# Layers 0, 1 and the first expert sums of a graph network: adjacency stationary, weights applied ahead, node phases inside the next block

## The chip, the cores and the metric

The kernel runs on one core of one Trainium2 chip. The metric is the device time in microseconds of one execution. The kernel before takes 2117.34 us, the median of three runs (2117.11 to 2117.92). Engines are called by the profile's names: PE is TensorE's matmul, PEld its weight load, DVE VectorE, ACT ScalarE, POOL GpSimd, SP SyncE; a name with a q behind it is that engine's sequencer, which issues DMAs and waits for semaphores.

## The reference

3125 nodes with 128 features, 100000 edges from `src` to `dst`. Two graph convolutions come first, then a network of three expert layers.

```python
# reference, shortened
def sage(x, src, dst, W_l, b_l, W_r):
    summed = segment_sum(x[src], dst, 3125)
    cnt = segment_sum(ones, dst, 3125)
    return summed / maximum(cnt, 1.0)[:, None] @ W_l + b_l + x @ W_r
h = relu(sage(x, src, dst, W_l0, b_l0, W_r0))           # layer 0
x = layernorm(x + sage(h, src, dst, W_l1, b_l1, W_r1))  # layer 1

h = x @ W_in + b_in                                     # 128 to 256 features
for l in range(3):                                      # layers 2, 3, 4
    agg = segment_sum(h[src], dst, 3125) / clip(deg, 1.0)
    logits = concat([h, agg]) @ router_W[l] + router_b[l]
    vals, idx = top_k(logits, 2); gates = softmax(vals)  # 2 of 8 experts
    weak = relu(agg @ weak_W[l] + weak_b[l])             # experts 0 to 3
    strong = relu(agg @ strong_W1[l] + strong_b1[l]) @ strong_W2[l] + strong_b2[l]
    moe = sum over the 2 chosen experts of gate * expert(agg)
    h = h + sigmoid(h @ conf_W[l] + conf_b[l]) * moe
return layernorm(x + h @ W_out + b_out)
```

All five layers sum the features of a node's sources over the same edges.

## The kernel before

Nodes are padded to 25 tiles of 128 (S = 25, P = 128). A block is 5 tiles, 640 nodes (TB = 5, BN = 640), and there are 5 blocks (NB = NK = 5).

**Start (to about 389 us).** TensorE multiplies zeros 64 times (L1414). Edges are then ranked by keys (products L1423 to L1427, VectorE L750 to L761), and one-hot products build the adjacency, the count of edges from each source to each target, as bf16 in SBUF (L1450 to L1457, evictions L1264 and L1266).

**Layers 0 and 1.** For each block of 640 target nodes, the adjacency comes in five pieces, each with the sources of five tiles: `ring[:, k, s]` is 128 sources x 640 targets. In layer 0 VectorE and ScalarE lay the pieces out from the adjacency in SBUF (`lay_out`, L407) and SP stores each to the DRAM array `adj_d`; layers 1 and 2 load them from there. The features are fp32, split into three bf16 parts, high, middle and low, which add up to them (`hs`). A part of 128 sources x 128 features is stationary in TensorE, and half of the piece's tile, 320 targets, moves: six sums a source tile, into two PSUM banks (L1480). Layer 0 also needs the number of edges of each target, so a tile of ones is stationary for two more products a source tile (L1485). The aggregate so comes out with the features on the partitions.

After the last sum comes the block's node phase, with TensorE waiting: VectorE forms the reciprocal of the counts over 640 columns (L862 to L864) and scales the sums (L870); TensorE transposes the block's own features (L1523) and multiplies them with W_r and the aggregates with W_l, ten fp32 products (L1531, L1532); VectorE adds the bias, applies the maximum with zero in layer 0, or the residual and layernorm (L920 to L948) in layer 1, and splits the result in three parts. GpSimd stores features and parts to DRAM (`h1_d`, `x1_d`, `split_d`), and the next layer loads the parts from `split_d` before its first sums. The input x is stored to `x_d` and loaded from there a block at a time.

**Layer 2 (first expert sums).** Sums as in layer 1 (L1564), over the 128 features of x. `first_turn` transposes x; `input_block` turns the reciprocals (L1675), forms the router's logits (nine columns, L1678 and L1679) and multiplies with W_in, 256 columns, for the nodes and for the aggregates (L1686). VectorE chooses two experts (L1014 to L1032), the ranks of rows in each expert come from TensorE (L1555), the positions from VectorE (L979 to L993), and GpSimd scatters each node's aggregate twice into rows sorted by expert (L669). VectorE makes the slot tables in the last block (L1076 to L1134).

**Slots and layers 3, 4.** A slot is a group of rows of one expert: SP loads it (L556), TensorE transposes (L1696) and multiplies with the expert's weights (L1707, L1718). The sums of layers 3 and 4 (L1590) have the adjacency as the stationary operand.

Every engine works its own list in the order in which it is written, and waits are semaphores; a waiting instruction holds all behind it on its engine. SP issues loads and stores in the written order.

## Time and profile before

| | us | share of the span |
|---|---|---|
| profiled execution | 2116.81 | |
| its span | 2115.0 | |
| PE busy | 1825.8 | 86% |
| PEld busy | 1473.9 | 70% |
| DVE busy | 904.5 | 43% |
| ACT busy | 775.9 | 37% |
| POOL busy | 627.9 | 30% |

The mean granted TensorE clock is 0.891 of full speed; HBM carries 130 GB/s over the span. Busy shares are means over stages with different limits, so the stages are read apart, by the chain of waits and the timeline. An fp32 matmul shows as two records.

### The profile page before, as it was taken

Reading aid. Unit: us, or ns where it says so; the run is one execution under the profiler, and the core shown is the slowest. Engines: PE = TensorE matmul, PEld = TensorE weight load, DVE = VectorE, ACT = ScalarE, POOL = GpSimd, SP = SyncE. Lnnn points to the kernel's source line nnn. Section 1 sums busy time; section 2 is a strip of 40 time slices with the busy share of each in tenths; the row PEclk is TensorE's granted clock in tenths of the full one; section 3 lists DMA queues with packets and bytes.
Section 4 is the critical chain, followed back from the end, with each engine's and each line's share of the span. In section 5 each row is a group of like instructions: output and inputs, shape, how many; then the busy total and the mean of one; then the engine's idle time right before and its main releaser. Section 6 shows DMA issues by size and latency. Waiting matters only on the chain.

```text
span 2115.0 us, 32510 instructions
## 1 busy us (share of the span) xinstructions
PE 1825.8 (86%) x10660; PEld 1473.9 (70%) x10662; DVE 904.5 (43%) x2470; ACT 775.9 (37%) x1257; POOL 627.9 (30%) x608
## 2 busy tenths in 40 slices
PE   7756666589889799899996999899996998999975
PEld 3545555466667577788885878788885887888864
DVE  6779999553423332543332111443332123433324
ACT  5356666521101010133334565333335554233321
POOL 1234444200000023264442031354440113454430
PEclk7766666799999899899998999899998999899986
DMA  6960000434656786254446753254446742344442
GB/s 151 340 233 0 0 0 0 180 147 162 178 172 239 233 295 206 92 95 73 71 71 193 244 188 101 67 92 73 76 63 222 269 147 97 78 83 73 71 106 63
DMA packets 183593, 277.35 MB, mean 131 GB/s; under 512 B 47551, under 2 KB 152693, under 8 KB 183362
## 3 DMA queue, kind: packets, MB, share of 16 engines
q1 hardware_dynamic: 145186, 217.47, 32.0%
q0 software_dynamic: 38304, 58.53, 15.3%
q8 instruction: 61, 1.00, 0.2%
q14 instruction: 42, 0.34, 0.1%
HBM read 158.82 MB, written 117.13 MB: 130 GB/s over the span
## 4 chain that ended last, share of the span: by engine, by line
PE 76%; DVE 13%; issue 5%; ACT 3%; DMA 2%; DVEq 1%; SPq 0%; POOL 0%; POOLq 0%; ACTq 0%
PE psum L1707 16%; PE psum L1718 16%; PE psum L1590 13%; PE psum L1480 9%; DVE arena L794 7%; PE psum L1564 5%; PE psum L1649 2%; PE psum L1696 2%; PE psum L1457 2%; PE psum L1485 2%; PE psum L1686 1%; PE psum L1425 1%; PE psum L1455 1%; PE psum L1740 1%; DVE arena L863 1%
## 5 line engine op out<-in xcount | busy, mean ns | idle before, releaser
L697 POOL DMA_INDIRECT h_rows<-arena,idx x192 | 310.7, 1618 | 409.6 <-DVE arena L1179 380.4
L1707 PE MATMUL psum<-arena 128*128 128x256 f32 x1536 | 357.4, 386 | 6.0 <-ACT arena L1364 6.0
L1367 ACT ACTIVATE arena<-psum,b1c 128x256 f32<-128x256 f32 x384 | 182.2, 474 | 476.7 <-PE psum L1707 476.5
L1718 PE MATMUL psum<-arena 128*128 x1536 | 347.4, 379 | 0.0
L1707 PEld LDWEIGHTS psum<-arena 128*128 128x128 f32 x1536 | 278.4, 191 | 69.7 <-ACT arena L1367 17.9
L1718 PEld LDWEIGHTS psum<-arena 128*128 128x128 f32 x1536 | 284.6, 190 | 34.8
L794 DVE TENSOR_TENSOR arena<-arena 125x1200 bf16<-125x1200 bf16 (+1 forms) x300 | 282.1, 1007 | 24.9 <-PE psum L1457 24.3
L669 POOL DMA_INDIRECT xs_d<-arena,pos x150 | 145.3, 969 | 407.8 <-DVEq L994 365.7
L1177 DVE TENSOR_TENSOR arena<-psum,arena 128x256 f32<-128x256 f32 x192 | 80.9, 421 | 414.6 <-PE psum L1718 414.6
L1480 PE MATMUL psum<-arena 128*128 128x320 bf16 x1500 | 226.7, 303 | 24.5 <-DVE arena L835 15.8
L623 POOL TENSOR_TENSOR arena<-arena 128x100 bf16 x200 | 134.5, 672 | 245.6 <-ACT arena L1264 241.8
L1480 PEld LDWEIGHTS psum<-arena 128*128 128x128 bf16 x1500 | 148.5, 99 | 84.0 <-issue 24.8
L1590 PE MATMUL psum<-halves,wide_a 128*128 128x512 f32 x625 | 161.3, 402 | 18.4 <-ACT wide_a L1327 17.3
L1590 PE MATMUL psum<-halves,wide_b 128*128 128x512 f32 x625 | 161.5, 403 | 18.1 <-ACT wide_b L1327 17.0
L1266 ACT CAST arena<-psum 128x800 f32 x200 | 165.6, 828 | 0.2 <-issue 0.2
L1590 PEld LDWEIGHTS psum<-halves,wide_a 128*128 128x128 f32 x625 | 114.2, 190 | 41.2 <-issue 19.9
L1590 PEld LDWEIGHTS psum<-halves,wide_b 128*128 128x128 f32 x625 | 114.3, 190 | 40.9 <-issue 19.6
L1457 PEld LDWEIGHTS psum<-arena 125*128 125x128 bf16 x1200 | 122.9, 134 | 24.8
L1457 PE MATMUL psum<-arena 125*128 125x100 bf16 x1200 | 139.7, 270 | 0.0
L1450 PE MATMUL psum<-arena 128*128 128x2 bf16 x200 | 37.4, 187 | 112.9 <-DVE arena L794 92.0
L1450 PEld LDWEIGHTS psum<-arena 128*128 128x128 bf16 x200 | 21.8, 109 | 128.7 <-issue 71.9
L1455 PE MATMUL psum<-arena 125*128 125x200 bf16 (+1 forms) x400 | 108.3, 368 | 0.0
(274 smaller groups left out, 2056.9 us busy)
## 6 DMA issues: line engine op xcount, KB each, us to landing
arena<-adj_d SPq DMA_DIRECT2D x50, 800.0 KB, 6.1
ring<-adj_d SPq DMA_DIRECT2D x50, 800.0 KB, 4.5
xs_d<-zrow SPq DMA_DIRECT2D x8, 3432.0 KB, 26.9
arena<-xs_d SPq DMA_DIRECT2D x96, 264.0 KB, 2.8
adj_d<-arena SPq DMA_DIRECT2D x25, 800.0 KB, 3.3
h_rows<-zrow SPq DMA_DIRECT2D x1, 8192.0 KB, 39.3
h_new<-h_rows SPq DMA_DIRECT2D x12, 640.0 KB, 8.2
arena<-x_d SPq DMA_DIRECT2D x20, 320.0 KB, 3.6
```

Source lines behind the costliest of these rows:

```text
L623: pool.tensor_tensor(a, first_w[:, u % 8], a, ALU.add).then_inc(s_first, 1)
L669: pool.indirect_dma_start(xs_d, bass.IndirectOffsetOnAxis(ap=pos[:, k, t:t + 1], axis=0), pay[:, k, t], None).then_inc(a_scat, 16)
L697: pool.indirect_dma_start(h_rows, bass.IndirectOffsetOnAxis(ap=idx[:, j % 2, h:h + 1], axis=0), ybuf[:, j % 2, h], None, compute_op=ALU.ad ...
L794: v.tensor_tensor(oh, every, keys.rearrange("p (n o z) -> p n o z", z=2, o=1).broadcast_to(shape), ALU.is_equal).then_inc(ready, 1)
L1266: act.copy(adj[:, bass.ds(off[u] + WC, G * WC)].rearrange("p (b n) -> p b n", b=2), banks[:, :, WC:WC + GA]).then_inc(s_wide, 1)
L1367: act.activation(hid[:, j % 2, f], psum[:, 5 + f % 2, 0:M], ACT.Relu, bias=b1c[:, bass.ds(at_b1[j % LOAD] + f, 1)]).then_inc(b_hidf, 1)
L1455: pe.matmul(bank[:, 0:cols], oh1[:, q, n, :, z % 2], ohe[:, q % 2, g, 0:cols, z], start=(z == 0), stop=False, skip_group_check=True)
L1457: mm = pe.matmul(bank[:, bass.ds(rel[(q % 2 * k + g) * (G - NST) + z - NST], WC)], oh1[:, q, n, :, z % 2], oh2[:, q, (g * (G - NST) + z - ...
L1480: mm = pe.matmul(psum[:, h, 0:HN], hs[:, k * SK + s, part, 0:P], half(ring[:, k, s], h), start=(k == 0 and s == 0 and part == 0), stop=(k ...
L1590: return pe.matmul(psum[:, t, :], adj32[piece_no(p, b, k) % 2][:, s, t * P:(t + 1) * P], halves[:, k * SK + s].rearrange("p k f -> p (k f) ...
L1707: mm = pe.matmul(psum[:, 5 + f % 2, 0:M], w1s[:, j % 2, f // 2, kt, f % 2 * P:(f % 2 + 1) * P], xsT[:, j % 2, kt], start=(kt == 0), stop=( ...
L1718: mm = pe.matmul(psum[:, h, 0:H], hid[:, j % 2, f, h * P:(h + 1) * P], w1f[:, bass.ds(at_w2 + f * H, H)], start=(f == 0), stop=(f == FT - 1))
```

## The change

All five parts concern the time before the slots of layer 2.

- **Warm-up:** 110 products of zeros in place of 64.
- **Gather (`gather`, all three layers):** the piece's tile, 128 sources x 128 targets, is stationary, and the three parts of the sources' features move together, 384 columns, into the PSUM bank of the target tile; five banks, one for each tile of the block. In layer 0 a column of ones behind them gives the count (385 columns). ScalarE takes each tile's sums out (`evicted`), in layers 1 and 2 scaled by the reciprocal count; VectorE adds the three parts (`block_of_nodes`).
- **Weights ahead:** for layers 0 and 1 a block's features are transposed (`turn_tiles`) and multiplied with W_l and W_r side by side, 256 columns (`multiply_tile`), before the gather. The left half is split in three parts and gathered; the right half, with the bias, waits in SBUF. In layer 2 the products have W_in and the router's ten columns, 266.
- **Node phases inside the next block:** the transposes and products are cut in three stages, which `beside` puts behind the source tiles named in PLACES (piece, tile), for the layer of which the block's nodes are made. The first two blocks of nodes of layer 0 go ahead of its first sums, the other three between the pieces of its first block.
- **No DRAM between:** parts stay in SBUF (`parts0`, `parts1`, used in turn); `split_d`, `h1_d` and `x_d` go. x comes in five chunks, VectorE lays out four of the first five pieces (FIRST_DVE), and rows to be scattered have two buffers in layer 2 (`pay_of`). The early part of the slot tables comes one block sooner.

```diff
+FIRST_DVE = (0, 2, 3, 4)
...
+        parts0 = carve([S, FW], BF16)
+        sums = carve([TB, FW], F32)
+        turned4 = carve([4, P], F32)
+        rest = carve([TB, D], F32)
         assert used[0] <= BN * SK * NK
+        used[0] = BN * SK * NK
+        parts1 = carve([S, 3 * D], BF16)
+        z1 = carve([S, D], F32)
+        assert used[0] <= 2 * BN * SK * NK
+        features = (parts0, parts1, parts0)
...
+            for k in range(NK):
+                for o, i in x_rows(chunk(x_all, k), k):
+                    sp.dma_start(o, i).then_inc(s_x[k], 16)
+                if k == 0:
+                    for o, i in ((wlr[0][:, 0:D], Wl0), (wlr[0][:, D:2 * D], Wr0)):
+                        sp.dma_start(o, i).then_inc(s_w0, 16)
...
-            def split_in(p):
...
-                pool.dma_start(split_d[:, bass.ds(b * TB, TB), :, 0:D].rearrange("p t k d -> p (t k) d"),
...
+            def products_split(n, t):
+                u = unit(n, t)
+                z = chunk(z0 if n < NB else z1, n % NB)
+                bank = psum[:, 6 + u % 2]
+                v.wait_ge(n_high, u + 1)
+                if n and t == 0:
+                    v.wait_ge(n_feat, n)
+                v.tensor_tensor(z[:, t], bank[:, D:2 * D], bl_b, ALU.add)
+                v.tensor_tensor(rest[:, t], bank[:, 0:D], parts_of(n)[:, t, 0], ALU.subtract).then_inc(n_taken, 1)
+            def low_part(n):
+                v.wait_ge(n_mid, n + 1)
+                v.tensor_tensor(parts_of(n)[:, :, 2], rest, parts_of(n)[:, :, 1], ALU.subtract).then_inc(n_feat, 1)
+            def block_of_nodes(p, b):
+                here, r = chunk(z0 if p == 0 else z1, b), rcol[:, b * TB:(b + 1) * TB]
+                a = sums[:, :, 0:D]
+                v.wait_ge(n_out, TB * (NB * p + b + 1))
+                if p == 0:
+                    d = sums[:, :, 3 * D]
+                    link(v.tensor_scalar(deg[:, 0], d, 1.0, None, ALU.max))
+                    link(v.reciprocal(deg[:, 1], deg[:, 0]))
+                    link(v.scalar_tensor_tensor(r, d, 1.0, deg[:, 1], ALU.min, ALU.mult))
+                link(v.tensor_tensor(sums[:, :, D:2 * D], sums[:, :, D:2 * D], sums[:, :, 2 * D:3 * D], ALU.add))
+                link(v.tensor_tensor(a, a, sums[:, :, D:2 * D], ALU.add))
+                if p == 0:
+                    for t in range(TB):
+                        ins = v.scalar_tensor_tensor(a[:, t], a[:, t], r[:, t:t + 1], here[:, t], ALU.mult, ALU.add)
+                    link(ins)
+                    link(v.tensor_scalar(a, a, 0.0, None, ALU.max))
+                elif p == 1:
+                    link(v.tensor_tensor(a, a, here, ALU.add))
+                    v.wait_ge(s_ldr, 16 * (b + 1 + (b == NB - 1)))
+                    link(v.tensor_tensor(rblk, rblk, a, ALU.add))
+                    layernorm(b)
+                v.nop().then_inc(n_node, 1)
...
+                    if b == (NB - 2 if p == 2 else NB - 1):
...
+            def evicted(i, t):
+                act.wait_ge(s_agg, TB * i + t + 1)
+                if i < NB:
+                    act.copy(sums[:, t, 0:3 * D + 1], psum[:, t, 0:3 * D + 1]).then_inc(n_out, 1)
+                else:
+                    c = i % NB * TB + t
+                    act.activation(sums[:, t, 0:3 * D], psum[:, t, 0:3 * D], ACT.Copy, scale=rcol[:, c:c + 1]).then_inc(n_out, 1)
...
-            for _ in range(64):
+            for _ in range(110):
...
-                    def summed(k, h, s):
-                        for part in range(3):
-                            mm = pe.matmul(psum[:, h, 0:HN], hs[:, k * SK + s, part, 0:P], half(ring[:, k, s], h),
-                                           start=(k == 0 and s == 0 and part == 0), stop=(k == NK - 1 and s == SK - 1 and part == 2))
...
+            def turn_tiles(n, g):
+                source = chunk(x_all, n) if n < NB else sums[:, :, 0:D] if n < 2 * NB or n >= 3 * NB else rblk
+                if 2 * n + g:
+                    pe.wait_ge(n_turned, 2 * n + g)
+                if n < NB:
+                    pe.wait_ge(s_x[n], 32 if n == NB - 1 else 16)
+                else:
+                    pe.wait_ge(n_node, n - NB + 1)
+                for t in ((4,) if g else range(4)):
+                    mm = pe.transpose(psum[:, 5, t % 4 * P:(t % 4 + 1) * P], source[:, t], ident[:, :])
+                mm.then_inc(n_turn, 1)
+            def multiply_tile(n, t):
+                u = unit(n, t)
+                weights = wlr[n // NB] if n < 2 * NB else w_ins[:, n // NB - 2, 0:H + 10]
+                pe.wait_ge(n_turned, 2 * n + 1 + t // 4)
+                if u >= 2:
+                    pe.wait_ge(n_taken, u - 1)
+                pe.matmul(psum[:, 6 + u % 2, 0:weights.shape[1]], turned4[:, t % 4], weights, start=True, stop=True).then_inc(n_mult, 1)
+            def turned_and_multiplied(n, stage):
+                if stage == 0:
+                    turn_tiles(n, 0)
+                elif stage == 1:
+                    multiply_tile(n, 0)
+                    turn_tiles(n, 1)
+                    multiply_tile(n, 1)
+                else:
+                    for t in range(2, TB):
+                        multiply_tile(n, t)
+            PLACES = (((1, 1), (1, 4), (2, 4)), ((2, 4), (3, 2), (3, 4)), ((0, 4), (1, 1), (1, 4)))
+            def gather(p, b):
+                i = NB * p + b
+                width = 3 * D + (1 if p == 0 else 0)
+                def summed(k, s, t):
+                    return pe.matmul(psum[:, t, 0:width], ring[:, k, s, t * P:(t + 1) * P], features[p][:, k * SK + s, 0:width],
+                                     start=(k == 0 and s == 0), stop=(k == NK - 1 and s == SK - 1))
...
+                for k in range(NK):
+                    if p == 0:
+                        pe.wait_ge(s_rel[k], b + 1)
+                        if b == 0 and k < NK - 1:
+                            if k:
+                                for stage in range(3):
+                                    turned_and_multiplied(k + 1, stage)
+                    else:
+                        pe.wait_ge(s_ring[k], (NB * (p - 1) + b + 1) * 16)
+                    pe.wait_ge(n_feat, NB * p + k + 1)
+                    if k < NK - 1:
+                        for s in range(SK):
+                            for t in range(TB):
+                                if i and k == 0 and s == 0:
+                                    pe.wait_ge(n_out, TB * (i - 1) + t + 1)
+                                mm = summed(k, s, t)
+                            if s == SK - 1:
+                                mm.then_inc(s_piece, 1)
+                            beside(k, s)
+                    else:
+                        for t in range(TB):
                             for s in range(SK):
...
+                                mm = summed(k, s, t)
+                            mm.then_inc(s_agg, 1)
...
+            pe.wait_ge(s_ones, 1)
+            for n in range(2):
+                for stage in range(3):
+                    turned_and_multiplied(n, stage)
+            for b in range(NB):
+                gather(0, b)
...
-                        first_aggregate(b)
-                        first_turn(b)
-                        input_block(b)
+                        gather(2, b)
...
+                    for stage in range(3):
+                        turned_and_multiplied(4 * NB - 1, stage)
```

Named in the rows below are the lines of the changed kernel: L1455 is `turn_tiles`, L1464 `multiply_tile`, L1484 `gather`. TensorE's order at the start of layer 0, before:

```order
L1495 REGISTER_ALU [waits aggregates_taken]
L1480 MATMUL psum<-arena 128x320 [waits x_split,piece_laid_out_0]
L1480 MATMUL psum<-arena 128x320 x5
L1485 MATMUL psum<-arena,ones_s 128x320 x2
L1480 MATMUL psum<-arena 128x320 x6
```

and after the change:

```order
L1455 MATMUL psum<-ident,arena 128x128 [waits count_columns_set,new_windows_copied,x_in_0,first_weights_in,tables_ready]
L1455 MATMUL psum<-ident,arena 128x128 x3
L1464 MATMUL psum<-arena 128x256 [waits turned_tiles_taken]
L1455 MATMUL psum<-ident,arena 128x128 [waits x_in_0,turned_tiles_taken]
L1464 MATMUL psum<-arena 128x256 [waits turned_tiles_taken]
L1464 MATMUL psum<-arena 128x256 [waits products_taken,turned_tiles_taken] x3
L1455 MATMUL psum<-ident,arena 128x128 [waits x_in_1,turned_tiles_taken]
...
L1464 MATMUL psum<-arena 128x256 [waits products_taken,turned_tiles_taken] x4
L1484 MATMUL psum<-arena 128x385 [waits features_ready,piece_laid_out_0]
L1484 MATMUL psum<-arena 128x385 x24
L1455 MATMUL psum<-ident,arena 128x128 [waits x_in_2,turned_tiles_taken,piece_laid_out_1]
```

The sums stood first; now ten transposes and ten products stand before them, and five more of each behind the first piece of 25 sums. TensorE's order in a block of layer 2, before (L1635 transposes of x, L1675 turned reciprocals, L1678 and L1679 logits, L1686 products with W_in), from the last piece on:

```order
L1564 MATMUL psum<-arena 128x320 [waits splits_in_4,piece_in_4]
L1564 MATMUL psum<-arena 128x320 x29
L1635 MATMUL psum<-ident,arena 128x128 [waits expert_residual_in]
L1635 MATMUL psum<-ident,arena 128x128 x4
L1675 MATMUL psum<-ident,arena 128x1 [waits router_products_taken,expert_aggregates_taken,turned_taken]
L1675 MATMUL psum<-ident,arena 128x1 x4
L1678 MATMUL psum<-arena 128x9
L1679 MATMUL psum<-arena 128x9
...
L1686 MATMUL psum<-arena 128x256 x5
L1686 MATMUL psum<-arena 128x256 [waits node_major_groups_taken]
```

and after, from the first piece of the second block of layer 1 on, in which the first block's nodes are made:

```order
L1484 MATMUL psum<-arena 128x384 [waits sums_evicted,features_ready,piece_in_0]
L1484 MATMUL psum<-arena 128x384 [waits sums_evicted] x4
L1484 MATMUL psum<-arena 128x384 x20
L1484 MATMUL psum<-arena 128x384 [waits features_ready,piece_in_1]
L1484 MATMUL psum<-arena 128x384 x24
...
L1455 MATMUL psum<-ident,arena 128x128 [waits nodes_ready,turned_tiles_taken,router_products_taken]
L1455 MATMUL psum<-ident,arena 128x128 x3
L1484 MATMUL psum<-arena 128x384 [waits features_ready,piece_in_3]
L1484 MATMUL psum<-arena 128x384 x14
L1464 MATMUL psum<-arena 128x266 [waits products_taken,turned_tiles_taken]
L1455 MATMUL psum<-ident,arena 128x128 [waits nodes_ready,turned_tiles_taken]
L1464 MATMUL psum<-arena 128x266 [waits products_taken,turned_tiles_taken]
L1484 MATMUL psum<-arena 128x384 x10
L1464 MATMUL psum<-arena 128x266 [waits products_taken,turned_tiles_taken] x3
L1484 MATMUL psum<-arena 128x384 [waits features_ready,piece_in_4]
```

The node phase stood behind all sums; now the transposes stand behind 15 source tiles of the next block and the products behind 18 and 20. On VectorE, the end of a layer-0 block before (L862 to L864 reciprocals of the counts, L870 scaling, L875 bias, L878 maximum):

```order
L862 TENSOR_SCALAR arena<-psum 128x320 [waits banks_aggregated]
L863 RECIPROCAL arena<-arena 128x320 [waits vector_steps]
L864 SCALAR_TENSOR_TENSOR arena<-psum,arena 128x320 [waits vector_steps]
L862 TENSOR_SCALAR arena<-psum 128x320
L863 RECIPROCAL arena<-arena 128x320 [waits vector_steps]
L864 SCALAR_TENSOR_TENSOR arena<-psum,arena 128x320 [waits vector_steps]
L870 TENSOR_TENSOR arena<-psum,arena 128x320 [waits aggregates_taken,banks_aggregated] x2
L407 COPY arena<-arena 128x640 [waits banks_aggregated,piece_stored_4]
L407 COPY arena<-arena 128x640 x4
L875 TENSOR_TENSOR arena<-psum,arena 128x384 [waits items_for_vector]
L875 TENSOR_TENSOR arena<-psum,arena 128x256 [waits items_for_vector]
L878 TENSOR_SCALAR arena<-arena 128x640 [waits items_taken_by_vector]
```

and after (L810 to L812 reciprocals, L813 and L814 the three parts added, L817 scaling, L819 maximum):

```order
L810 TENSOR_SCALAR deg<-arena 128x5 [waits piece_laid_out_3,piece_laid_out_4,piece_laid_out_2,sums_evicted,piece_laid_out_1,piece_laid_out_0]
L811 RECIPROCAL deg<-deg 128x5 [waits vector_steps]
L812 SCALAR_TENSOR_TENSOR rcol<-arena,deg 128x5 [waits vector_steps]
L813 TENSOR_TENSOR arena<-arena 128x5x128 [waits vector_steps]
L814 TENSOR_TENSOR arena<-arena 128x5x128 [waits vector_steps]
L817 SCALAR_TENSOR_TENSOR arena<-arena,rcol 128x128 [waits vector_steps]
L817 SCALAR_TENSOR_TENSOR arena<-arena,rcol 128x128 x4
L819 TENSOR_SCALAR arena<-arena 128x5x128 [waits vector_steps]
L408 COPY arena<-arena 128x640 [waits vector_steps,tiles_aggregated,piece_stored_4]
```

The reciprocals shrink from 320 columns twice to 5, and the additions of the three parts are new.

## Rows read from the trace of the kernel before

**Rows 1.** The page, chain that ended last: its shares by engine.

```profile
PE 76%; DVE 13%; issue 5%; ACT 3%; DMA 2%; DVEq 1%; SPq 0%; POOL 0%; POOLq 0%; ACTq 0%
```

**Rows 2.** Chain of waits, pieces in order of time: start us, us, what.

```profile
586.94 22.75 PE psum L1480 x150
...
686.10 20.38 PE psum L1480 x150
...
721.13 3.58 PE psum L1547 x16
...
893.60 3.80 PE psum L1707 x16
901.48 3.52 PE psum L1707 x16
...
1148.14 30.10 PE psum L1590 x125
```

**Rows 3.** Timeline, start of layer 0: start, busy us, instructions, [idle before, releaser].

```profile
389.03 4.14 DVE L407 COPY arena<-arena 128x640 bf16<-128x640 bf16 x15 [5.29 <-ACT arena L1266]
...
403.41 1.76 PE L1480 MATMUL psum<-arena 128*128 128x320 bf16 x6 [15.75 <-DVE arena L835]
```

**Rows 4.** Timeline, warm-up and the first two rounds of keys.

```profile
2.27 16.70 PE L1414 MATMUL psum<-arena 128*128 128x512 bf16 x63 [2.27 <-POOL arena L606]
...
30.44 0.59 PE L1423 MATMUL psum<-arena 1*125 1x400 bf16 x1 [11.47 <-DVE arena L750]
...
46.12 0.57 DVE L761 TENSOR_TENSOR arena<-psum,arena 125x400 f32<-125x400 f32 x1 [13.03 <-PE psum L1427]
...
54.70 0.57 DVE L761 TENSOR_TENSOR arena<-psum,arena 125x400 f32<-125x400 f32 x1 [0.91 <-PE psum L1427]
```

**Rows 5.** Windows: length, busy (x) of the five engines, PEclk, DMA share, GB/s.

```profile
18.00:20.00 2.00, 0.97 (x5) 0.24 (x3) 2.00 (x1) 2.00 (x1) 0.00 (x0) 1.00 0.13 6
20.00:22.00 2.00, 0.00 (x0) 0.00 (x0) 1.90 (x4) 2.00 (x1) 0.00 (x0) 0.86 0.11 3
...
470.00:472.00 2.00, 2.00 (x11) 2.00 (x11) 0.16 (x2) 0.00 (x0) 0.00 (x0) 0.50 0.60 253
...
752.00:778.00 26.00, 26.00 (x175) 19.27 (x174) 9.01 (x46) 2.75 (x3) 4.75 (x6) 0.94 1.06 368
```

**Rows 6.** Instruction groups by line: | busy us, mean ns | idle before, releaser.

```profile
L1480 PEld LDWEIGHTS psum<-arena 128*128 128x128 bf16 x1500 | 148.5, 99 | 84.0 <-issue 24.8
...
L1264 ACT CAST arena<-psum 128x100 bf16<-128x100 f32 x200 | 48.8, 244 | 119.5 <-PE psum L1457 117.7 <-POOL arena L623 0.2
...
L1177 DVE TENSOR_TENSOR arena<-psum,arena 128x256 f32<-128x256 f32 x192 | 80.9, 421 | 414.6 <-PE psum L1718 414.6
```

**Rows 7.** Timeline, products at the end of layer 0's first block.

```profile
435.88 0.49 PE L1531 MATMUL psum<-arena 128*128 128x128 f32 x2 [2.78 <-DVE arena L870]
```

**Rows 8.** Timeline, VectorE at the end of a layer-1 block.

```profile
638.31 0.82 DVE L920 TENSOR_TENSOR arena<-arena 128x640 f32<-128x640 f32 x1
...
641.47 1.37 DVE L948 TENSOR_SCALAR arena<-arena 128x128 f32<-128x128 f32 x5
```

**Rows 9.** The page, DMA issues: xcount, KB each, us to landing.

```profile
arena<-x_d SPq DMA_DIRECT2D x20, 320.0 KB, 3.6
```

**Rows 10.** Timeline, end of layer 2 and start of the slots.

```profile
867.66 0.17 DVE L1076 TENSOR_TENSOR arena<-nxt,cap 128x8 f32<-128x8 f32 x1
...
868.35 0.98 POOL L669 DMA_INDIRECT xs_d<-arena,pos  x1 [15.56 <-DVEq L994]
...
875.85 0.16 DVE L1134 TENSOR_SCALAR arena<-arena 1x12 int32<-1x12 f32 x1
...
883.01 20.26 SPq L556 DMA_DIRECT2D arena<-xs_d  x4
...
891.01 0.66 PE L1696 MATMUL psum<-ident,arena 128*128 128x128 f32 x4 [0.93 <-DVE arena L1061]
```

**Rows 11.** Timeline, one of the last products of the kernel.

```profile
2088.84 4.63 PE L1740 MATMUL psum<-arena 128*128 128x128 f32 x20 [0.46 <-ACT arena L1406]
```

816 lines of the change are left out of this document (328 added, 488 removed).

## The prediction

> **What bounds the kernel now.** I read the chain of waits by engine first, then its pieces in order of time, then the stages between them in the timeline. The chain is 76% TensorE [rows 1], so a microsecond is won where TensorE stands idle, streams columns that need not exist, or runs at its lower clock. The pieces give the stages [rows 2]: layer 0 runs until layer 1 starts at 586.94, layer 1 until about 710, layer 2 (the first expert sums) from 721.13, and the slots of the first expert layer start at 893.60. Layer 0 starts at 403.41, when the first MATMUL follows 15.75 us of idle [rows 3]. So the three gathering layers take 893.60 - 403.41 = 490.2 us. Behind 893.60 the change alters nothing that costs time (semaphores and places of buffers only), so that part is to move as a block.
>
> **The key stage (64 to 110 warm-up matmuls).** TensorE warms up from 2.27 to 18.97, then idles 11.47 us and starts the keys at 30.44; the first of four rounds ends at 46.12, the second 8.58 us later, at 54.70 [rows 4]. The first lasts 15.7 us, since the granted clock is at its lower level when it starts: it was 1.00 in 18 to 20, and fell within 20 to 22 (mean 0.86, so some 2.4 us after the last matmul) [rows 5]. 46 matmuls more of 512 columns, at 2.4 GHz 213 ns each, end at about 28.8; the gap shrinks to 1.6 us, less than the 2.4 us that the clock lasted. The first round then takes 8.6 instead of 15.7: 7.1 us are won, since VectorE and ScalarE wait for TensorE in it. If the clock falls anyway, 0. I take 7.1.
>
> **The gather.** Before, a piece of five source tiles takes per tile six sums and, in layer 0, two counts of 320 columns. In layer 1, 150 sums take 20.38 us: 135.9 ns for one [rows 2], which is 320 columns at 2.4 GHz (133.3) and 2.6 ns. After, a block is 125 matmuls of 384 columns (385 in layer 0, the last is the count): 162.6 to 163 ns, 20.4 us. Layers 1 and 2 gain nothing from it (750 x 320 = 625 x 384 columns); layer 0 loses its 250 counts. The weight load has a mean of 99 ns [rows 6], under 163, and stays hidden.
>
> The Trainium skill, page "TensorE: Matmul & The Clock Gate", section "Back-to-back issue gap", has a rule that would give more: in a stream of load and matmul pairs, 81 ns at 128 columns and 131 ns at 512. Interpolated, 384 columns would take about 114 ns, and 1875 of them 92 us less than below. By the same rule 320 columns would take 106 ns; the trace has 135.9, so the trace disagrees and the sum goes by it.
>
> **The node phase.** In layer 1 a block lasts 24.2 us: the chain's pieces end at 586.94 + 22.75 and 686.10 + 20.38, four blocks apart [rows 2]. So its node part costs TensorE 3.8 us: five transposes, ten fp32 products of 128 columns, and short waits. The new node part has the same columns (five transposes, five products of 256 or 266), placed in three stages inside the next block. It costs 3.8 again if nobody is late. In layer 0 the old node part costs more: VectorE's reciprocals over 640 columns hold TensorE 2.78 us [rows 7], and these go (the new one has 5 columns). In layer 2 five blocks and the end took 893.60 - 721.13 = 172.5, or 34.5 each: nine-column products, twenty products of 256 columns, and waits.
>
> Who might be late: layer 0, TensorE wants the tiles after seven source tiles, 7 x 0.82 = 5.7 us. Last eviction 0.6, three small steps 0.6, two adds over 640 columns 2 x 0.86, five tiles 1.4, the maximum 0.5: ready at about 4.9, slack 0.8. Layer 1, wanted after 15 tiles, 12.2: eviction 0.7, three adds 2.6, then the residual add and layernorm, which take 638.31 to 642.84 = 4.5 before [rows 8]: 7.8, slack 4. Layer 2, wanted at 4.1: 0.7 and 2 x 0.86, slack 1.6. The third product stage waits about 0.5 us for banks 6 and 7 in every block; that is inside the 3.8, as the old waits were. What is queued behind a late stage is the whole next piece of sums, and behind a late ScalarE the next evictions.
>
> So a block is 20.4 + 3.8 = 24.2; without any wait 23.3, and with 2 to 3 us of late chains 27.
>
> **Layer 0, start.** VectorE now lays out four of five pieces: 20 copies at 4.14/15 = 0.276 [rows 3], ready at 394.5. The first chunk of x, 320 KB, issued at 391.4, takes 3.6 us as such a block does now [rows 9], the weights are queued behind: about 396. Then two blocks of nodes go through turn, copy, product, high part, two VectorE steps, all exposed and at the lower clock. Transposes and their copy 2.0; then per tile a product (a warm record of 256 columns is 3.52/16 = 0.22, two records a tile, cold 0.9 [rows 2]), a cast (0.24) and two VectorE steps (0.55, from 0.42 for 256 columns) [rows 6]; two banks, so two tiles per round trip: 5.4 from the first product. Block 0 of nodes: 396 to 403.4; the second 8.0: TensorE gathers from 411.4, against 403.4: 8 us lost (bounds 5 and 14).
>
> Block 0 then has three more such stages in it, which TensorE walks through in order. Each is 5.6 us at the upper clock: transposes and copy 1.5, and 4.1 for the five products with their round trips. Sums: 4.1 a piece, 6.1 for the first, half of it cold as now. 6.1 + 3 x (5.6 + 4.1) + 4.1 = 39.3, and 1.5 for short falls of the clock: 40.8, until 452.2. Bounds 34 and 60.
>
> **Layer ends.** No store, load or split lies between layers any more: features are made block by block, four pieces ahead. Layer 0: 4 x 24.2 = 96.8, until 549.0. Layer 1: 5 x 24.2 and the 16 nine-column records, now 3.58 us cold [rows 2], warm half, with a switch 2.3: 123.3, until 672.3. Layer 2: 5 x 24.2 and 2.0 for ranks and the ten columns more: 123.0, until 795.3. The expert weights go out behind the pieces of block 1, and the pieces for block 2 queue behind them. Both together, 9.6 MB, took 26 us at 368 GB/s from 752 to 778 [rows 5]; they are wanted in pieces over 24 to 40 us: hidden.
>
> **The end of layer 2.** The last ranks stand 4.1 us before the gather ends. VectorE then takes 1.8 for the positions and 8.4 for the slot tables (867.66 to 876.0) [rows 10], so it is free 6.1 us behind the end, and two adds make the nodes ready at 7.9. Turn, copy, five cold products: 14.5. The other limit is the scatter: now from 868.35 to the load of sorted rows at 883.01, 14.7 [rows 10]; the new one starts 2.3 before the end, so the load goes at 12.4 and rows are in at about 15.5. The slot's first transposes follow, and the first product 2.6 later (891.01 to 893.60): 18 us, until 813.3. Bounds 15 and 22.
>
> **The sum.** 813.3 - 893.6 = -80.3, and -7.1 at the keys: -87.4. The profiled execution took 2116.81 with a span of 2115.0; 2116.8 - 87.4 = 2029.4. The median of the runs is 0.5 above it, so 2030.
>
> **Rivals.**
> 1. Block 0 runs cold. The stages with gaps between them keep TensorE half busy. For: the final projections, with gaps between them, run 20 records of 128 columns in 4.63 us, the lower clock [rows 11], and behind the same gap of the next block the clock stood at 0.50 (470 to 472) [rows 5]. Against: pieces of 4.1 us full work lie between, and the clock rose within 4 us of them at 403. Price: 125 sums at twice 163 are 20 us more, 15 products 6 more, less 3.5 already counted, and some of it warm: +18, 2048. Chance 0.17.
> 2. The node chains are late. The slack in layer 0 is 0.8 us by a sum of ten steps, each with a semaphore, and ScalarE lays out a piece between two turned copies. At 2 us in each of 14 blocks: +28, 2058. Chance 0.13.
> 3. The clock falls before the keys: +7, 2037. For: the gap is not zero. Chance 0.08.
> 4. Matmuls of 384 columns go as fast as their weight loads: 99 ns [rows 6] instead of 163, 1875 x 64 = 120 us less, 1910. Against: loads of 99 ns stand beside 135.9 ns for 320 columns [rows 2, 6]. The rule of the Trainium skill quoted above lies on this side, with its 114 ns. Chance 0.01.
> 5. Slower than before: with the adjacency stationary, each of 1875 matmuls pays its own weight load. If none is hidden, 99 ns x 1875 = 186 us, 2216; it decides from 47 ns a matmul. For: layers 3 and 4, in this orientation, take 30.10/125 = 241 ns for 512 columns [rows 2], 27 above 213. Against: that load is fp32, and the bf16 loads of 99 ns vanish under 136 now. Chance 0.03.
> A plan that does less than it says (a feature or piece late by a cycle of waits) has 0.02 more, somewhere up to 2110.
>
> **How the numbers follow.** The sum has 0.56: 2030, its own range 2014 to 2046, from the bounds above (start -3 to +6, block 0 -7 to +10, blocks -10 to +12, end -3 to +4, not all at once). The range of 8 in 10 takes in rivals 1 and 3 and most of 2: 2012 to 2060. A measurement tells 0.2% (4 us) from no change. Faster holds in all cases but rival 5 and a part of the last: 0.96; within 0.2%: 0.01; slower 0.03.
>
> **What would show it.** In the new profile: the first key round 8.6 us instead of 15.7; the first 385-column matmul about 1 us after 404 (411 less 7); block 0 of 41 us with three gaps; then 14 blocks of 24 us, each 125 matmuls at 163 ns, TensorE busy 95% or more and at clock 1.00; no gap between layers; 18 us from the last sum to the first slot's product; slots at 7.41 us apart as before. Wrong would be: matmuls at over 170 ns; TensorE waits for nodes_ready or features_ready of a microsecond or more in every block; a clock of 0.5 in block 0; a slower slot stage.

## The result, and the profile after

The changed kernel takes 2049.68 us, the median of four runs (2040.57 to 2053.5), against 2117.63 before: ratio 0.9656, 95% interval 0.9624 to 0.9687. Forecast were 2030, with a range of 2012 to 2060. So 68 us are won where 87 were forecast: inside the range of the forecast, above the 2014 to 2046 that its sum gave itself. The profiled execution took 2050.06 with a span of 2048.1 and a granted clock of 0.898 (before 0.891).

The page of the changed kernel, the chain's shares by engine [rows 1] and the gather's groups:

```profile
PE 76%; DVE 12%; issue 5%; ACT 3%; DMA 2%; DVEq 1%; SPq 1%; POOL 0%; ACTq 0%; POOLq 0%
...
L1484 PE MATMUL psum<-arena 128*128 128x384 bf16 (+1 forms) x1875 | 318.2, 327 | 0.5 <-ACT arena L1233 0.2
...
L1484 PEld LDWEIGHTS psum<-arena 128*128 128x128 bf16 x1875 | 181.9, 98 | 126.6 <-ACT arena L1236 3.3
```

TensorE is idle before its sums for 0.5 us in all, so the 1875 loads of 98 ns stand beside its matmuls. The pieces of the chain (start, us, what) that answer to [rows 2]:

```profile
416.22 4.09 PE psum L1484 x25
...
474.09 14.03 PE psum L1484 x85
...
498.14 14.03 PE psum L1484 x85
...
599.77 4.71 PE psum L1484 x29
...
623.54 4.71 PE psum L1484 x29
...
814.99 6.57 PE psum L1657 x16
825.65 3.52 PE psum L1657 x16
```

A piece of 25 sums takes 4.09, 163.6 ns each. Blocks are 24.05 us apart in layer 0 and 23.77 in layer 1. The stages, by where they end (before, forecast from the prediction's sum, after):

| end of | before | forecast | after | stage, forecast | stage, measured |
|---|---|---|---|---|---|
| adjacency (first layout copy starts) | 389.03 | 381.9 | 393.25 | -7.1 | +4.2 |
| node blocks ahead (first sum) | 403.41 | 404.3 | 416.06 | 22.4 | 22.8 |
| block 0 of layer 0 | | 445.1 | 452.8 | 40.8 | 36.7 |
| layer 0 | 586.94 | 541.9 | 554.5 | 96.8 | 101.7 |
| layer 1 | | 665.2 | 675.2 | 123.3 | 120.7 |
| layer 2's sums | | 788.2 | 795.1 | 123.0 | 119.9 |
| first slot product starts | 893.60 | 806.2 | 814.99 | 18.0 | 19.9 |
| span | 2115.0 | 2027.6 | 2048.1 | 1221.4 | 1233.1 |

Three rows carry the miss: the adjacency stage (11.3 us), layer 0 (4.9), and all that stands behind the first slot product (11.7), which was to move as a block. The other five together are 7.5 us shorter than forecast. The end of a layer is read from the eviction of its last sums (ScalarE, start us, busy us); in the timeline of the changed kernel these are the last ones of layers 0, 1 and 2:

```profile
554.48 0.48 ACT L1233 COPY arena<-psum 128x385 f32<-128x385 f32 x1 [0.34 <-PE psum L1484]
...
675.19 0.58 ACT L1236 ACTIVATE arena<-psum,rcol 128x384 f32<-128x384 f32 x1 [0.23 <-PE psum L1484]
...
795.12 0.58 ACT L1236 ACTIVATE arena<-psum,rcol 128x384 f32<-128x384 f32 x1 [0.24 <-PE psum L1484]
```

For block 0 of layer 0 it is the end of TensorE's last sum, 444.43 + 8.37 = 452.8, since ScalarE evicts late there: it lays out pieces of block 1 first.

```profile
444.43 8.37 PE L1484 MATMUL psum<-arena 128*128 128x385 bf16 x50
...
446.08 6.36 ACT L408 COPY arena<-arena 128x640 bf16<-128x640 bf16 x10
...
452.35 1.99 ACT L1233 COPY arena<-psum 128x385 f32<-128x385 f32 x5
```

The gain lies in two stretches of the table. Layer 0, from its first sum to its end, took 183.5 us before and takes 138.4; from there to the first slot product were 306.7 and are 260.5. Against these 91.3 us stand 4.2 more for the adjacency, 8.4 more ahead of the first sum and 11.7 more behind the first slot product. No run tests the turned gather or the missing trips to DRAM alone, so how the 91.3 divide between the parts of the change is read from the stages and not shown by experiment, but for the placing of the node phases.

**The keys.** Windows of the changed kernel (columns as in [rows 5]):

```profile
30.00:32.00 2.00, 1.69 (x9) 1.14 (x9) 2.00 (x7) 1.71 (x1) 0.00 (x0) 1.00 0.40 3
32.00:34.00 2.00, 2.00 (x8) 1.25 (x7) 0.95 (x3) 2.00 (x1) 0.00 (x0) 0.58 0.42 3
...
58.00:60.00 2.00, 2.00 (x8) 1.41 (x7) 0.00 (x0) 0.00 (x0) 0.00 (x0) 0.59 1.09 341
```

Its timeline, the first key product and VectorE's steps behind the first and the second round [rows 4]:

```profile
30.31 0.38 PE L1397 MATMUL psum<-arena 1*125 1x400 bf16 x1 [2.84 <-DVE arena L710]
...
44.85 0.57 DVE L721 TENSOR_TENSOR arena<-psum,arena 125x400 f32<-125x400 f32 x1 [11.89 <-PE psum L1401]
...
60.41 0.57 DVE L721 TENSOR_TENSOR arena<-psum,arena 125x400 f32<-125x400 f32 x1 [7.90 <-PE psum L1401]
```

The warm-up ended at 27.47, 1.3 sooner than forecast, the gap was 2.84 us and the keys started at the upper clock. But the clock fell at about 32.3, when TensorE was busy again, and came back at about 59.6 although TensorE was busy throughout: two rounds at the lower clock instead of one.

**Block 1 of layer 0.** The first product of layer 1's features, in the timeline of the changed kernel:

```profile
459.91 2.62 PE L1484 MATMUL psum<-arena 128*128 128x385 bf16 x15
...
465.00 0.70 PE L1464 MATMUL psum<-arena 128*128 128x256 f32 x2 [2.48 <-DMA arena<-in_L_gnn_b_l]
...
466.33 5.68 PE L1484 MATMUL psum<-arena 128*128 128x385 bf16 x25
```

It waits 2.48 us for layer 1's bias, which SP issues at 460.69, behind the wait for the layouts of this block. The clock falls behind the wait (0.95 in 464 to 466, 0.50 in 466 to 468), and 25 sums take 5.68 instead of 4.25.

**The end of layer 2**, timeline of the changed kernel [rows 10]:

```profile
803.29 1.09 PE L1455 MATMUL psum<-ident,arena 128*128 128x128 f32 x4 [8.21 <-DVEq L825]
...
809.35 1.58 SPq L530 DMA_DIRECT2D arena<-xs_d  x3
...
812.23 0.66 PE L1646 MATMUL psum<-ident,arena 128*128 128x128 f32 x4 [1.56 <-DMA arena<-xs_d]
...
814.99 6.57 PE L1657 MATMUL psum<-arena 128*128 128x256 f32 x16 [2.11 <-ACT arena L1338]
```

TensorE waits 8.21 us for the last block's nodes (forecast 7.9), and the slots start 19.9 us behind the last sum. Its first slot runs at the lower clock: 10.66 us to the next instead of 7.88 before.

**The slots.** Weight loads in the timeline of the changed kernel, around one slot's transposes (L1646):

```profile
877.69 1.70 PEld L1657 LDWEIGHTS psum<-arena 128*128 128x128 f32 x8
879.58 1.59 PEld L1657 LDWEIGHTS psum<-arena 128*128 128x128 f32 x8 [0.20 <-ACT arena L1341]
881.60 0.42 PEld L1646 LDWEIGHTS psum<-ident,arena 128*128 128x128 f32 x4 [0.42 <-issue]
```

Before, nearly every slot's first product came 7.41 us behind the last slot's; now every fourth comes 7.65 behind. That slot is the one before which TensorE loads four addresses from the slot tables into registers. In the order of instructions nothing had changed there.

### The profile page after: what moved, and what is told of

It reads as the page before. It is cut to its first block, busy times and chain, and to the rows that moved or that the text cites. A ratio compares the mean times of both kernels' runs of the same rounds, so it can differ in the third digit from the quotient of the medians.

```text
span 2048.1 us, 30902 instructions
## 1 busy us (share of the span) xinstructions
PE 1787.7 (87%) x9855; PEld 1380.5 (67%) x9858; DVE 892.3 (44%) x2593; ACT 829.3 (40%) x1388; POOL 618.4 (30%) x593
## 4 chain that ended last, share of the span: by engine, by line
PE 76%; DVE 12%; issue 5%; ACT 3%; DMA 2%; DVEq 1%; SPq 1%; POOL 0%; ACTq 0%; POOLq 0%
PE psum L1657 17%; PE psum L1668 16%; PE psum L1484 14%; PE psum L1571 13%; DVE arena L754 7%; PE psum L1623 2%; PE psum L1464 2%; PE psum L1646 2%; PE psum L1431 2%; PE psum L1399 2%; PE psum L1429 1%; PE psum L1690 1%; PE psum L1617 1%; ACT wide_b L1317 1%; ACT wide_a L1317 1%
## 5 line engine op out<-in xcount | busy, mean ns | idle before, releaser
L1484 PE MATMUL psum<-arena 128*128 128x384 bf16 (+1 forms) x1875 | 318.2, 327 | 0.5 <-ACT arena L1233 0.2
L754 DVE TENSOR_TENSOR arena<-arena 125x1200 bf16<-125x1200 bf16 (+1 forms) x300 | 282.0, 1006 | 23.6 <-PE psum L1431 23.0
L1484 PEld LDWEIGHTS psum<-arena 128*128 128x128 bf16 x1875 | 181.9, 98 | 126.6 <-ACT arena L1236 3.3
L1103 DVE TENSOR_TENSOR arena<-psum,arena 128x256 f32<-128x256 f32 x192 | 80.9, 421 | 381.9 <-PE psum L1668 380.8
L1424 PEld LDWEIGHTS psum<-arena 128*128 128x128 bf16 x200 | 21.6, 108 | 126.7 <-issue 81.2
## 6 DMA issues: line engine op xcount, KB each, us to landing
xs_d<-zrow SPq DMA_DIRECT2D x8, 3432.0 KB, 27.3
```

Source lines behind the costliest of these rows:

```text
L754: v.tensor_tensor(oh, every, keys.rearrange("p (n o z) -> p n o z", z=2, o=1).broadcast_to(shape), ALU.is_equal).then_inc(ready, 1)
L1484: return pe.matmul(psum[:, t, 0:width], ring[:, k, s, t * P:(t + 1) * P], features[p][:, k * SK + s, 0:width], start=(k == 0 and s == 0), ...
```

## The experiments

**130 warm-up matmuls.**

```diff
-            for _ in range(110):
+            for _ in range(130):
```

> The changed kernel with 130 warm-up matmuls in place of 110. In the changed kernel the warm-up ends at 27.46 us, TensorE idles 2.84 us, the keys start at 30.31 at the full clock, the clock falls at about 32.3 and is back only at about 59, so the first key round takes 14.5 us and the second 15.6 instead of 8.6 each. Theory: the idle gap makes the clock fall, although it falls after the gap. With 20 more matmuls (20 x 0.213 = 4.3 us) there is no gap, the first round ends at about 39 and all rounds take 8.6: 5.9 + 7.0 = 12.9 us less, 2037. Rival: the clock falls because of what the keys do (their products use 100 of 128 rows, and few rows in the first), gap or not: then it falls again at about 32 and the time stays at 2050.

Measured: 2044.42 (2041.47 to 2046.59), ratio to before 0.9634 (0.9605 to 0.9664), so some 5 us less and not 13. Windows of its trace:

```profile
32.00:34.00 2.00, 2.00 (x11) 1.31 (x11) 1.24 (x4) 2.00 (x1) 0.00 (x0) 1.00 0.41 3
...
58.00:60.00 2.00, 2.00 (x12) 1.30 (x11) 1.83 (x9) 0.00 (x0) 0.00 (x0) 1.00 1.09 341
```

The clock stays up through the keys and the adjacency stage starts at 71.0 instead of 82.5, 11.5 us earlier, as the theory has it. The rival is refuted: the same keys hold the clock. But the adjacency stage gives a third of it back. VectorE's first layout copy, which ends that stage, in the timelines of the changed kernel and of this run:

```profile
393.25 3.91 DVE L408 COPY arena<-arena 128x640 bf16<-128x640 bf16 x14 [5.25 <-ACT arena L1196]
...
385.41 2.73 DVE L408 COPY arena<-arena 128x640 bf16<-128x640 bf16 x9 [4.91 <-ACT arena L1196]
```

Of the 11.5 us, 7.8 are left there. The stage takes 310.7 us in the changed kernel and 314.4 here, and the profiles agree: 309.7 to 310.7 where it starts at 82.5 or later, 312.2 to 312.7 at 75.1 to 76.8, 313.6 to 314.7 at 69.9 to 72.3. VectorE's 200 steps in it (L754) are 1.66 us apart before 140 us in the changed kernel and 1.86 here, and 1.48 apart in both behind 150, where the DMA engines have gone quiet (busy share 1.09 in 100 to 120 and 0.01 in 140 to 160 of the changed kernel). So whoever starts earlier does more of the stage in its slow part; that the transfers make it slow is not tested. By the first slot product 6.7 us are left (808.28 against 814.99), and 3.2 are lost behind it, where a later paragraph has the scatter.

**64 warm-up matmuls.**

```diff
-            for _ in range(110):
+            for _ in range(64):
```

> The changed kernel with 64 warm-up matmuls, as before the change. Theory: the clock is low when the keys start and rises about 15 us later, inside the second round, as in the kernel before: the adjacency stage starts at about 76.8 instead of 82.5, and the whole is 5.7 us less, 2044: the 46 added matmuls cost time. Rival: when the clock rises is chance, and the place of the adjacency stage does not follow the number of warm-up matmuls: 2050. It also shifts TensorE's instructions by 46: if the 0.24 us that TensorE loses at every fourth slot (7.65 instead of 7.41) come from where its code lies, they go or move; if they come from the address of the slot table, they stay.

Measured: 2050.11 (2046.53 to 2051.85), no difference. The adjacency stage started at 84.8, since the clock rose at about 62 and not at 45 as in the profile before. So my theory fell: the 46 added matmuls are not what makes the lower clock last. The long register load stayed at every fourth slot (7.80 from transpose to transpose), so it isn't a matter of where TensorE's code lies.

**The kernel before with 110.**

> The kernel before with 110 warm-up matmuls in place of 64, that part of the change alone. Theory of the clock, as above: the keys start at the full clock, it falls 2 us later and comes back late, the adjacency stage starts 4 to 6 us later, 2122. If the late return is chance: between 2110 (no fall, 7 us won) and 2123.

Measured: 2118.62 (2114.43 to 2128.03, ten runs), ratio 0.9994 (0.9975 to 1.0013): this part alone is worth nothing that can be measured. Its adjacency stage started at 84.6. Over all profiles, that start lies at 76.8, 84.8 and 86.8 with 64 matmuls; at 69.9, 75.1, 76.6, 82.5, 84.2, 84.2, 84.6 and 86.5 with 110; and at 71.0, 71.2 and 72.3 with 130. With 110 the clock fell in seven of eight profiles, 2 to 5 us after the warm-up's end, and came back 10 to 31 us later; in three of the seven it fell at the very end of the gap and in four when the keys had started. The length of the gap does not sort them: it held over 2.69 us and fell with 1.83. With 130, and no gap, it did not fall before the keys' end in three of three.

**The slot tables moved by 8 bytes.**

```diff
+        used[0] += 4
         tabs = carve([6, SLOTS], I32, 1)
```

> The changed kernel with the slot tables' buffer moved by 8 bytes, to a multiple of 16 bytes as in the kernel before (the change moved it by 440 bytes, to 8 above a multiple of 16). TensorE loads four slot addresses into registers at every fourth slot; after the change the slot distance there is 7.65 instead of 7.41 us, in each of the three slot stages. Theory: the odd address makes that load slower; with the move all slots are 7.41 apart, 7 or 8 x 0.24 us less in each of three stages: 5.4 us less, 2044.5. Rival: the load is slower for another reason (order of the code, other engines' traffic): 2050.

Measured: 2045.92 (2036.73 to 2047.9), ratio 0.9649 (0.9619 to 0.968). Its timeline at such a slot (one more line in the code: L1647 is the slot's transposes, L1658 and L1669 its products):

```profile
867.55 1.60 PEld L1658 LDWEIGHTS psum<-arena 128*128 128x128 f32 x8 [0.20 <-ACT arena L1342]
869.17 0.57 PEld L1647 LDWEIGHTS psum<-ident,arena 128*128 128x128 f32 x4
869.72 3.32 PEld L1669 LDWEIGHTS psum<-arena 128*128 128x128 f32 x16
```

The distances of 7.8 between transposes, 21 before, are all gone; 84 of 95 are 7.4. The times alone would not show it (the interval takes in the changed kernel's ratio), the trace does. The same edit in the kernel before, which puts its table on an odd address:

> The kernel before with the slot tables' buffer moved by 8 bytes, from a multiple of 16 bytes to 8 above one. Theory, from the run with the buffer moved back (slots 7.41 us apart again): the odd address alone makes TensorE's register load at every fourth slot slower: its slot transposes come 7.8 us instead of 7.4 after the last there, 0.24 us net, 22 times, 5.3 us in all, 2123. Rival (the load is slower only in the changed kernel's surroundings): slots stay 7.41 apart, 2118.

Measured: 2129.16 against 2121.02 on the same chip, ratio 1.005 (1.0033 to 1.0066). The 7.8 appear, 21 times, with the same wait for "issue" (its timeline; L1697 is the slot's transposes):

```profile
965.29 1.60 PEld L1708 LDWEIGHTS psum<-arena 128*128 128x128 f32 x8 [0.20 <-ACT arena L1368]
967.30 0.42 PEld L1697 LDWEIGHTS psum<-ident,arena 128*128 128x128 f32 x4 [0.41 <-issue]
```

So it is shown from both sides that the address does it: 0.24 us each, 21 x 0.24 = 5.0 us in all. (The edit moves the buffers behind the table by 8 bytes too; the load that waits reads the table.) The rest of the 8 us is within the scatter of the key stage, which started at 86.8 in its profile.

**The bias by another queue.**

```diff
-                if b == 1:
-                    sp.wait_ge(n_taken, unit(NB, 0))
-                    sp.dma_start(bl_b, bl1.unsqueeze(0).broadcast_to((P, D))).then_inc(s_w1, 16)
...
+            pool.wait_ge(n_taken, unit(NB, 0))
+            pool.dma_start(bl_b, bl1.unsqueeze(0).broadcast_to((P, D))).then_inc(s_b1, 16)
             for k in range(NK):
                 pool.wait_ge(s_rel[k], NB)
```

> The changed kernel with layer 1's bias loaded from GpSimd's queue as soon as its place is free, in place of SP's queue behind the stores of adjacency pieces. In the changed kernel the first product of layer 1's features (at 465.0 us) waits 2.48 us for this load, the clock falls behind the wait, and the second block of layer 0 takes 29.5 us against 24.05 for the three after it. Theory: both go, the block takes 24.1: 5.4 us less, 2044. Rival: the block is longer because it is the first with all node stages (layouts by ScalarE late): the wait goes to another releaser and the block stays above 27.

Measured: 2044.04 (2037.04 to 2053.64), ratio 0.9633 (0.9608 to 0.9658). Its timeline, the same product and the sums behind it:

```profile
466.07 0.59 PE L1464 MATMUL psum<-arena 128*128 128x256 f32 x2
...
467.05 4.25 PE L1484 MATMUL psum<-arena 128*128 128x385 bf16 x25
```

The wait is gone and the clock stays up. From block 0's last sum to block 1's last are 25.1 us instead of 29.5: 4.4 of the 5.4 expected. The last 1.0 is ScalarE's: here too it lays out pieces for 6.36 us first, and the first sums of block 1 then wait for its evictions one by one.

**Node stages of layers 1 and 2 at the block's start.**

```diff
-            PLACES = (((1, 1), (1, 4), (2, 4)), ((2, 4), (3, 2), (3, 4)), ((0, 4), (1, 1), (1, 4)))
+            PLACES = (((1, 1), (1, 4), (2, 4)), ((0, 0), (0, 0), (0, 0)), ((0, 0), (0, 0), (0, 0)))
```

> The changed kernel with the node stages of layers 1 and 2 all placed behind the first source tile of the next block, as if the node phase came at a block's end; layer 0 unchanged. It prices the placing inside the block. Theory: TensorE then waits for the nodes: in layer 1 about 7 us (ready 7.8 us behind the block's end, wanted at 0.8) and some 2 us more for the turned tiles and between the products, five times, and the clock falls in part; in layer 2 about 2 us and 2 us four times: 5 x 9 + 4 x 4 = 61 us more, 2111, between 2095 and 2130. Rival: the interleaving hides little, since the node work is TensorE's own: under 15 us more.

Measured: 2120.21 (2115.72 to 2125.12, ten runs), ratio to before 0.9998 (0.9984 to 1.0012): 70 us more than the changed kernel, and all that the change had won is gone (expected 2111, between 2095 and 2130). In its timeline, behind the first block of layer 1:

```profile
590.21 1.09 PE L1455 MATMUL psum<-ident,arena 128*128 128x128 f32 x4 [7.46 <-DVEq L825]
592.97 1.25 PE L1464 MATMUL psum<-arena 128*128 128x266 f32 x2 [1.68 <-ACT arena L1216]
594.02 0.42 PE L1455 MATMUL psum<-ident,arena 128*128 128x128 f32 x1
594.23 3.37 PE L1464 MATMUL psum<-arena 128*128 128x266 f32 x8
```

The wait is 7.46 (expected 7), and the products behind it run at the lower clock. Blocks are then some 35 us apart in layer 1 and 27 in layer 2, against 23.8 and 24.0. How the 11 us of a block of layer 1 divide between waits and clock is not told apart.

**Matmuls in the two long waits.**

```diff
+            for _ in range(20):
+                pe.matmul(psum[:, 5, :], ones_s[:, :], adj[:, 70000:70512], start=True, stop=True)
             pe.wait_ge(s_w0, 48)
...
+                    for q in range(50):
+                        pe.matmul(psum[:, 5, 0:3 * D], ones_s[:, :], parts0[:, q % S, 0:3 * D], start=True, stop=True)
                     for stage in range(3):
```

> The changed kernel with matmuls whose results nobody reads in TensorE's two long waits: 20 of 512 columns while x and the weights are loaded (393 to 401 us) and 50 of 384 columns between the last sum and the last block's nodes (795 to 803 us). Theory: the clock is up when the work behind each wait starts: the first two node blocks (15.2 us from the first transpose to the first sum, at the lower clock) take about 11, and the products and the first slot (11.7 us from the first transpose at 803.3 to 815.0, and 10.7 for the first slot) save about 4: 8 us less in all, 2042. Rival: the clock isn't held by such work, or the waits between the products make it fall again: 2050; or the filling ends late and costs its lateness, up to 2 us each.

Measured: 2043.2 (2040.87 to 2044.4), ratio 0.9637 (0.9618 to 0.9656). From the first layout to the first sum are 20.5 us instead of 22.8. That the time lies near the 2042 expected is luck: only these 2.3 of the 8 us came, and in this profile the adjacency stage started 7.4 us earlier than in that of the changed kernel. At the end of layer 2 nothing is won:

```profile
793.88 0.63 PE L1459 MATMUL psum<-ident,arena 128*128 128x128 f32 x4
...
803.87 0.66 PE L1650 MATMUL psum<-ident,arena 128*128 128x128 f32 x4 [2.60 <-DMA arena<-xs_d]
805.59 6.63 PE L1661 MATMUL psum<-arena 128*128 128x256 f32 x16 [1.07 <-ACT arena L1338]
```

The last node block's transposes run at the upper clock, but the slot then waits for its rows, so the stage takes 19.9 as before; the gaps between make the clock fall again and the first slot takes 6.63 as well. The other limit that the prediction named, the scatter and the load of the sorted rows, decides once TensorE is earlier.

**Layout of the first pieces as before the change.**

```diff
-FIRST_DVE = (0, 2, 3, 4)
+FIRST_DVE = (0, 2, 4)
```

> The changed kernel with the layout of the first pieces as before: VectorE three (0, 2, 4), ScalarE two (1, 3). Theory: nothing waits for the layouts, since x and the weights arrive 7.4 us behind the layouts' start and ScalarE ends its two in 6.4: from the first layout to the first sum 22.8 us as in the changed kernel. Rival: ScalarE is late for the first turned tiles, and the stage is up to 3 us longer.

Measured: from the first layout to the first sum 23.2 us, against 22.7 in the unaltered kernel beside it and 21.5 to 23.1 in the other profiles with this stage unaltered. So the layouts cost at most some tenths of a us there, which one profile can't tell from none. Its time, 2124.56, comes from a series of runs in which the kernel before took 2196.65; only ratios and stages from there are used. Both this series and one three minutes later ran on the chip numbered 13, and in the later one the kernel before took 2122.75. So the chip as the reason, as I expected it for the last run below, is not shown, and why the kernels were slower there stays open. The two profiles there with the change as it is and with this edit have blocks of 24.05 and 23.77 us like all others in layers 0 and 1; the last three blocks of layer 2 are the first longer ones (26.6 to 29.7 instead of 24.0).

**Four repairs together, and the changed kernel beside it.**

> The changed kernel with four repairs together: 130 warm-up matmuls, the slot tables' buffer back on a multiple of 16 bytes, layer 1's bias by GpSimd's queue, and 20 unread matmuls of 512 columns while x and the weights are loaded. By the parts: keys at the full clock (against their mean of a few profiles: 6 to 12 us less, here 8), tables 5.3, bias 5.4 of which 4 showed in its profile, filling 2.3: 19.6 us less than the changed kernel, 2030. Rival: the granted clock gives back elsewhere what it gives here, and the parts don't add: 2036 to 2042.

> The changed kernel once more, unaltered, on the same chip as the version with the four repairs. If the scatter of its four runs (2040.6 to 2053.5) is when the clock rises in the key stage, its runs spread again over some 13 us, and the adjacency stage starts anywhere between 70 and 87 us. Median expected 2049, as measured; if the repairs' gain is a matter of the chip, it is near 2035.

Measured in that series: a ratio to before of 0.9533 (0.9475 to 0.9591) against 0.9703 (0.9655 to 0.9752). The intervals don't meet. The medians are 2099.11 (five runs; a sixth took 2113.63) and 2132.51, 33 us apart. The first slot product came at 809.0 and 829.6.

> The version with the four repairs once more, since the chip of its first run granted less clock to every kernel (kernel before 2196.7). On a chip like the others: 2030 by the sum of the parts, 2036 to 2042 if they don't add.

Measured: 2027.19 (2025.72 to 2031.77), ratio 0.956 (0.9532 to 0.9587), against 0.9656 for the change as it is. The parts add: 2030 was the sum, and the medians of the four single runs lay 5.3, 3.8, 5.6 and 6.5 us below the changed kernel's, 21.2 together, against 22.5 here. This version beats both kernels.

## Why the prediction was right or wrong

**What bounds it, and the rest as a block.** That TensorE's idle time, columns and clock are what counts held. That the part behind the slots' start moves unchanged did not: it grew from 1221.4 to 1233.1. Of the 11.7 us, 5.0 are the slot tables' address, shown both ways. I had written that places of buffers cost no time: that was the step that failed. The other 6.7 are 2.8 for the first slot at the lower clock, 1.6 in the last stage, 1.5 for a longer load of a piece (6.35 against 4.85 us) and 0.8 without a place, and none of these is shown to come from the change. The first slot ran at the lower clock in all profiles with the change, but also in one of the three without it (the kernel before with its table moved). The same load takes 4.40 to 6.73 us in eight profiles with the change and 4.85, 4.88 and 5.60 in those without. The whole part took 1232.8 to 1237.5 in six profiles with the table at its odd address, 1230.6 with the table alone moved back, 1225.4 with the four repairs, and without the change 1221.4, 1225.1 with 110 warm-up matmuls and 1231.2 with the table moved: it scatters by some 4 us with the same instructions. A slower slot stage, which the prediction had named as a sign of being wrong, so came. From the last slot of one expert layer to the last of the next, twice, are 457.2 and 457.3 us before, 459.1 and 460.8 in the changed kernel and 457.8 and 457.7 with the repairs.

**The keys, -7.1.** Wrong: +4.2 in the profile. The step that failed is "the gap shrinks to 1.6 us, less than the 2.4 us that the clock lasted". The gap was 2.84, since the clock rose sooner in the warm-up than in the profile before (at 5.0 us and not at 7.8). Above all, a gap that ends before the clock falls does not save it: the clock fell 2 us after the keys had started. Rival 3, given 0.08, is what happened, and it is worse than its price of 7, as the lower clock lasted two rounds. With 110 the part wins or loses by chance, and in the kernel before it is worth nothing on average. A second step failed with it: that what the keys win is won for good. In the one profile with 110 matmuls in which the clock held, the adjacency stage started 6.9 us earlier than before, but ended only 4.4 earlier (384.61 against 389.03); with 130 it ended 3.6 earlier. So the term was too large even where its mechanism worked.

**The gather.** Right: 163.6 ns for 385 columns against 163 forecast. Rivals 4 and 5 fall: the loads of 98 ns are hidden under the matmuls, neither adding to them nor limiting them.

**The node phase inside the next block.** Right within 0.4 us a block: 24.05, 23.77 and 24.03 against 24.2. Rival 2 falls; no stage is late but for 0.2 to 0.5 us at the last product, as named. The run with the stages of layers 1 and 2 at the block's start shows what their placing is worth: as much as the whole gain.

**Start of layer 0 and block 0.** The 8 us lost ahead of the first sum came out (22.8 against 22.4). Block 0 took 36.7 instead of 40.8: its sums ran at the upper clock from the first piece on, since the clock rose in 412 to 416 (mean 0.67, so at about 414.6), and stayed up through the three stages with their gaps of 0.5 to 0.7 us (1.00 throughout 416 to 453). So the first piece took 4.1 and not 6.1, and the 1.5 for falls of the clock was not needed. Rival 1 falls.

**Layer 0, 96.8.** 101.7 measured. The mis-sized term is a wait the sum did not have: the second bias, 2.48 us behind SP's queue, and a clock that falls behind it, 4.4 us together, and 1.0 for evictions that ScalarE makes late. I had looked at who issues the pieces, not at what was queued behind them for the next layer.

**Layers 1 and 2, and the end.** 120.7 and 119.9 against 123.3 and 123.0: the blocks 0.4 shorter, the nine-column products 1.5 instead of 2.3, and no extra wait in layer 2. The end, 19.9 against 18, lies inside its bounds; when the last products were made sooner, the load of sorted rows held the slots back just as long.

So the direction held, and of the mechanisms all but that of the keys. The 20 us between 2030 and 2050 are the keys (11.3) and the part behind the slots' start (11.7), with the rest cancelling. With the four repairs the kernel takes 2027, but that it so meets the 2030 is in part luck: its adjacency stage still ends 3.9 us later than forecast (385.78 against 381.9) and the part behind the slots' start is 4.0 longer, while everything between is 11.0 shorter, 2.3 of them by the filling, which the forecast did not have.

## What to carry to other kernels

Work that an engine has to wait for is best put inside the next block's stream, at a place worked out from the chain that makes it ready: here this is worth 70 us in 2050. When buffers are rearranged, look at the addresses of the small tables that sequencers read: an address 8 bytes off cost 5 us in code that nobody had touched. A warm-up that ended 2 to 5 us before the work held the clock in one profile of eight, and one that ran into the work in three of three, so judge such a part by several profiles of the stage, not by one. And look at the end of the next stage too before you book what one has won: here a third was gone by then.

## What the runs showed of the hardware

- A register load of four 4-byte values by TensorE's sequencer from a table in SBUF held it 0.24 us longer when the table lay 8 bytes above a multiple of 16 than when it lay on one (7.65 against 7.41 us a slot, seen in both kernels by moving the table).
- The granted clock can fall while TensorE is fully busy: in 32 to 34 us of the changed kernel it went from 1.00 to 0.50, 5 us after the start of a gap of 2.84 us that had already ended. It then stayed at 0.50 for 27.3 us of unbroken work, and for 10 to 31 in the other profiles with 110 warm-up matmuls in which it fell.
- bf16 matmuls of 385 moving columns with a new stationary operand each took 163.6 ns in a long stream, its columns at 2.4 GHz and 3 ns; the loads of 98 ns cost nothing.
